# VectorE a block ahead in a graph-attention edge loop: weighting, additions and logits in another order, six row slots instead of four

## The reference, cut to what matters

```
h = einsum('nd,hdf->nhf', x, W)                     # 4 heads of 64
e = leaky_relu(a_src[src] + a_dst[dst], 0.2)        # one logit an edge and head
ex = exp(e - emax[dst])
out = segment_sum(h[src] * ex / denom[dst], dst)
```

## Time and profile before

| | us |
|---|---|
| median of 3 runs | 2905.74 |
| lowest, highest | 2902.65, 2912.12 |
| profiled execution, its time | 2900.4 |
| its span (first to last instruction) | 2898.3 |
| busy POOL, PE, DVE, ACT | 1778.3, 1655.7, 1538.2, 687.3 |

### The profile page before, as it was taken

How to read it: one execution, slowest core, us unless ns; L and a number is a source line. 1 busy time by engine, 2 the same in 40 slices (tenths; PEclk the granted TensorE clock), 3 DMA queues, 4 the chain that set the end, 5 groups by cost and what they waited for, 6 DMA issues and landing times. The chain is left out here.

```text
span 2898.3 us, 56530 instructions
## 1 busy us (share of the span) xinstructions
PE 1655.7 (57%) x17359; PEld 1267.0 (44%) x17359; DVE 1538.2 (53%) x5813; ACT 687.3 (24%) x2082; POOL 1778.3 (61%) x1803
## 2 busy tenths in 40 slices
PE   6566664556566334443443366765666666557894
PEld 5334433434444223332332344554554454346783
DVE  5544445556666444544544555565564655453443
ACT  4222221112221112122122123224322233323220
POOL 1666666666666666666666665656566666645774
PEclk9666565655555555555555566777777667668997
DMA  9356555534454453365365467667656765547987
GB/s 297 109 163 166 163 159 152 174 96 124 122 155 116 118 127 104 96 181 149 107 175 152 135 179 220 177 187 210 195 161 198 219 205 147 158 125 218 250 235 207
DMA packets 317811, 480.53 MB, mean 166 GB/s; under 512 B 77671, under 2 KB 241593, under 8 KB 312893
## 3 DMA queue, kind: packets, MB, share of 16 engines
q0 software_dynamic: 90960, 237.28, 31.2%
q1 hardware_dynamic: 217420, 231.05, 25.9%
q10 hardware_dynamic: 9120, 8.49, 0.9%
HBM read 399.71 MB, written 110.47 MB: 176 GB/s over the span
## 5 line engine op out<-in xcount | busy, mean ns | idle before, releaser
L1264 POOL DMA_INDIRECT region<-node_table,src_idx x1612 | 1573.9, 976 | 926.4 <-remote 489.0
L1454 PE MATMUL ps_p<-region 128*32 128x65 f32 x12896 | 405.9, 293 | 779.6 <-DVE region L1702 614.0
L1454 PEld LDWEIGHTS ps_p<-region 128*32 128x32 f32 x12896 | 311.6, 153 | 884.6 <-DVE region L1702 690.5
L1710 DVE SCALAR_TENSOR_TENSOR acc<-ps_p,region,acc 128x65 f32 x806 | 192.9, 280 | 805.1 <-remote 750.4
L1330 ACT ACTIVATE ps_p<-region 128x16 f32<-128x16 f32 x403 | 75.5, 187 | 1033.7 <-DVE region L1696 553.3
L1326 ACT ACTIVATE region<-ps_s 128x128 f32<-128x128 f32 x403 | 111.3, 276 | 835.3 <-PE ps_s L1436 384.5
L1436 PE MATMUL ps_s<-ident,region 128*128 128x128 f32 x403 | 170.2, 422 | 215.2 <-DVE region L1696 120.7
L1702 DVE TENSOR_TENSOR region<-region,ps_p 128x512 f32<-128x512 f32 x403 | 273.3, 678 | 24.0 <-ACT ps_p L1330 11.9
L1440 PEld LDWEIGHTS ps_s<-region 128*128 128x128 f32 x806 | 215.5, 294 | 75.4 <-issue 49.9
L1436 PEld LDWEIGHTS ps_s<-ident,region 128*128 128x128 f32 x403 | 105.6, 262 | 238.2 <-DVE region L1696 132.8
L1440 PE MATMUL ps_s<-region 128*128 128x32 f32 x806 | 191.0, 327 | 6.7 <-issue 6.6
(11 more groups left out here) (371 smaller groups left out, 2663.0 us busy)
## 6 DMA issues: line engine op xcount, KB each, us to landing
region<-in_W_dram SPq DMA_DIRECT2D x84, 512.0 KB
expert_in<-run_rows SPq DMA_DIRECT2D x280, 130.0 KB
region<-node_table,src_idx POOLq DMA_INDIRECT x1612
acc<-in_W_dram SPq DMA_DIRECT2D x28, 512.0 KB
region<-expert_in SPq DMA_DIRECT2D x47, 260.0 KB
acc<-base_rows SPq DMA_DIRECT2D x13, 896.0 KB
qkv_rows<-region SPq DMA_DIRECT2D x49, 194.0 KB
y_rows<-acc SPq DMA_DIRECT2D x28, 256.0 KB
```

Source lines behind the costliest of these rows:

```text
L1264: pool.indirect_dma_start(out=rows[:, s, j, :], out_offset=None, in_=table[:, :], in_offset=bass.IndirectOffsetOnAxis(ap=src_idx[:, n * SU ...
L1454: m = pe.matmul(ps_p[s % 2][h * WIN:(h + 1) * WIN, 0:HC], wts[:, s % 2, j, h, :], rows[:, s, j, h * HC:(h + 1) * HC], start=j == 0, stop=j ...
L1710: m = dve.scalar_tensor_tensor(out=a, in0=ps_p[s % 2][:, 0:HC], scalar=here[:, k, at(n)], in1=a, op0=ALU.mult, op1=ALU.add)
```

## The change

Three things change in the edge loop. `SL` is 6, so six blocks of gathered rows fit, and POOL may start block `n` when the sums of `n - 6` are done. The region grows for it. DVE's order in a body becomes `weigh(n)`, `accumulate(n - 1)`, `logits(n + 1)`, `prepare(n + 3)`, with `logits(0)` ahead of the loop. And `accumulate` uses the register that `prepare` filled, where it loaded the column a second time. One more edit leaves out a call in a stage that is entered only where the destinations are not sorted as expected, which these inputs don't do. The orders of PE, ACT and SP and the waits of each function stay.

```diff
-REGION = 15300
+REGION = 17500
...
-    SL, ML = 4, 4
+    SL, ML = 6, 4
...
+            column_of = {}
+
             def prepare(n, s):
-                c = dve.value_load(column[0:1, at(n)], min_val=0, max_val=ACC_C - 2)
+                c = column_of[n] = dve.value_load(column[0:1, at(n)], min_val=0, max_val=ACC_C - 2)
...
             def accumulate(n, s):
-                c = dve.value_load(column[0:1, at(n)], min_val=0, max_val=ACC_C - 2)
+                c = column_of.pop(n)
                 dve.wait_ge(block_ps, n + 1)
                 dve.wait_ge(block_done, n)
...
             def body(n, s, ahead=3):
-                logits(n, s)
-                if not isinstance(n, int) or n >= 1:
+                weigh(n, s)
+                if n:
                     accumulate(n - 1, (s + SL - 1) % SL)
-                weigh(n, s)
+                if n + 1 < BLOCKS:
+                    logits(n + 1, (s + 1) % SL)
                 if ahead == 3 or n + 3 < BLOCKS:
                     prepare(n + 3, s + 3)
...
             dve.wait_ge(zeroed, 4)
+            logits(0, 0)
```

More of the change, by code:

```diff
@@ L1999, in round_of @@
                 def round_of(k):
-                    if k == EARLY - 1:
-                        part.sums(sp, early_round(k, 1))
                     for u in ROW_STEPS:
```

## The result

The changed kernel takes 2923.5 us (median of 7 runs, 2916.9 to 2934.2), the kernel before 2906.0 in the same comparison (7 runs). The ratio is 1.0066, with a 95% interval of 1.0055 to 1.0078: slower by 0.7%, where 2715 us were forecast. The profiled execution took 2926.2 us, with a span of 2924.5; before it was 2898.3.

What follows compares the result with a forecast made beforehand. Bound: finished blocks' reports held until POOL's gathers pause, about 6 us a block. Two reports per silence give -131 us (first 260 blocks) and -53 (last 140), other parts nothing: 2900.4 to 2716, forecast 2715 us; 8-in-10 range 2500 to 2870.

Steps and rivals of the forecast that it cites:

- The reading of the bound: Edge loop: a finished block's report is held until POOL stops issuing gathers, giving a 5.97 us period.
- One silence of POOL then reports two blocks: DVE's new order lets PE queue two blocks' sums: 5.49 us a block, 0.5 less; -131 and -53 us.
- Rival E: The late report is PE's own work, sums take up to 4.97 us, no gain: 2895 us; chance 0.05.
- Rival B: No silence is needed any more, POOL's issuing bounds the edge loop at 5.16 us a block: 2535 us; chance 0.20.
- The second load: Load ahead of DVE's additions goes (42 us idle); `prepare`'s load may show 0 to 266 us; costed at nothing.
- The logits a block earlier: DVE's logits of n + 1 need only gathered rows, so wait for nothing; up to 0.4 us less, taken as 0.
- Six slots: POOL issues 24 gathers before its first wait, not 16; first report 10 us later with two blocks: nothing net.
- Rival C: One report a silence, edge-loop period stays 5.97, only what is over it falls: 2860 us; chance 0.20.
- Rival D: Slower: longer gather runs delay single reports by 2.0 us, period 6.9; 3000 us with 160 such blocks; chance 0.10.

Runs made afterwards that it cites:

- pair_wait: Changed kernel with POOL waiting only ahead of every second block, for both blocks' sums, so it issues eight gathers per silence; 3110.6 us, 1.0717 of the kernel before.
- after_again: Changed kernel rerun unchanged on chip 12, where sums are not stretched; 2601.1 us against 2548.8 for the kernel before, ratio 1.0195.

## Why the prediction was wrong

- *The reading of the bound* held in its numbers (four gathers, 1.26 us idle, 4.97 us from first matmul to report) and failed in its sense: "the work is done, its report waits for POOL's silence". The records that end after 1.09 us are modelled. In the changed kernel the later matmuls come into PE only haltingly, at 1094.62 to 1096.91 and for 17 us at the start: PE is at work on the block. This is the step that failed. In its place the runs show sums that take 4.8 us beside three gathers and 6.1 beside four, so that a DVE that is ahead gains nothing.
- *"One silence of POOL then reports two blocks", 5.49 us a block, -184 us.* With PE stretched, four gathers and one block's sums take 0.91 + 4 x 1.29 = 6.07 us however early the sums are queued; the median period is 6.1 still. Forced by `pair_wait` it came out at 12.54 us for the pair shown, 6.27 a block, where 5.49 was the forecast, and at 3110.6 us in all.
- *Rival E* (0.05: the late report is PE's own work, no gain, 2895) was nearest in mechanism and time. It was turned down because of the earlier trace rows, where the same matmuls took 1.39 us. That row had no gather beside it. It refuted that the matmuls are slow by themselves; it could not refute that gathers make them slow. The rule cited there (the Trainium skill, "Trainium Architecture — The Big Picture", section "What this means for kernel authors") that engines run apart unless a semaphore ties them is contradicted by the rows here, and they decide: on the prediction's chip and on chips 3, 7 and 11 PE's sums have a median of 1.14 us with less than half a gather beside them and of 4.8 us beside about three, with no semaphore between the two in that time. On chips 5 and 12 the traces agree with the rule (1.14 us beside gathers).
- *Rival B* (2535) has the time of the kernel before on a chip without stretching (2541.6). That is a coincidence of numbers: B had the change bring it about, and there the change costs 2%.
- *The second load, cost 0 in sum:* its removal was worth 0.4%. That the load in `prepare` would show was in the text (0 to 266 us, hidden); it does show, 0.6 us a block, and by `after_again` it counts where DVE isn't waiting for PE.
- *The logits a block earlier, "this waits for nothing":* only the gathered rows were looked at. They also wait for L1440, and behind the linear attention's matmuls that cost 10 to 11 us between blocks 104 and 132.
- *Six slots, "nothing net":* 10.9 us late at the first report, near the 10 us worked out, and never made up, since no later silence reports two blocks.
- *Rival C's* sum is off by a little: 260 blocks at 5.97 are 1552 us, 43 under 1595 and not 35.
- *Rival D* had the sign, with another mechanism and a price (94 us over the kernel before) five times too high; six slots did lengthen POOL's run at the start, once.

## What to carry to other kernels

A duration that was seen with one neighbour silent says nothing of the same work beside that neighbour: before a late report is called held, look for a trace in which the worker is fed early, or count what its queue still takes. When a step is moved ahead, every semaphore that it waits for has to be traced to its place in the other engine's queue, and a load that a long instruction hid has to be moved with its cover. And where one chip decides a size of this kind, time the kernel before on more than one.

## What the runs showed of the hardware

- The same program takes 2904 to 2942 us on the chips of the prediction's comparison, 3, 7 and 11, and 2542 to 2549 on chips 5 and 12: 14 to 16% apart. Chip 5 was measured twice, with 0.3% between. Whether chip 3 and the prediction's are the same isn't told by the results, so the stretching was seen on three or four chips. What in a chip, or beside it at the time, makes the difference is not known.
- Where there is stretching, a block's sums take 1.14 us with less than half a gather beside them, 4.77 us beside about three and 6.09 us beside four, whether a gather moves 135 or 34 KB, and at either level of the clock. Eight matmuls in place of sixteen, or four of 128 columns, are stretched too, but fewer blocks of them. Whether it is POOL's issuing or what the DMA engines do for the gathers is not settled.
- It goes on after the gathers' issue: PE was through 1.1 us after the end of the last of three, 1.8 after the last of eight (`pair_wait`), and 2.9 after the last of eleven (the changed kernel's start).
